# The shared network's first products moved between the last weightings and the tables, in TensorE's order

## The reference, cut to what matters

```python
xn = _layernorm(x)
# attention: softmax of masked scores, times the values
s = softmax(causal(q @ k.T / 16)) @ v
# router: softmax of 8 logits, 2 best groups of 4, then 2 best experts of those
weights, topk_idx = ...
counts = jnp.bincount(topk_idx.reshape(-1), length=E)
flat_idx = topk_idx.reshape(-1)
routed_in = xf[flat_idx] * weights
# which rows go through which expert follows from counts alone
h = silu(_grouped_mm(routed_in, w1, counts)) * _grouped_mm(routed_in, w3, counts)
routed_out = _grouped_mm(h, w2, counts)
# shared network
shared = silu(xf @ sw1.T) * (xf @ sw3.T) @ sw2.T
out = shared.at[flat_idx].add(routed_out)
x = x + s * silu(out)
```

## Time and profile before

| what | value |
|---|---|
| median of 3 runs | 239.04 us (238.71 to 239.35) |
| the profiled execution's own time | 240.62 us |
| its span, first to last instruction | 238.6 us |
| TensorE busy | 230.6 us (97%) |
| TensorE's weight loads | 205.8 us (86%) |
| VectorE, ScalarE, GpSimd busy | 186.8, 144.9, 55.4 us |
| mean granted TensorE clock | 0.993 |

### The profile page before, as it was taken

One profiled execution on the slowest core, in us unless ns is written; L12 is line 12 of the kernel. 1 busy time (PEld: TensorE's weight loads), 2 busy tenths in 40 slices (PEclk: granted clock), 3 DMA queues, 4 the chain that ended last, 5 costly groups with the idle time before them and its releaser, 6 DMA issues.

```text
span 238.6 us, 4677 instructions
## 1 busy us (share of the span) xinstructions
PE 230.6 (97%) x1533; PEld 205.8 (86%) x1533; DVE 186.8 (78%) x620; ACT 144.9 (61%) x392; POOL 55.4 (23%) x108
## 2 busy tenths in 40 slices
PE   7898999999999999999999999999999999999983
PEld 5788998998989989999899998898988889898843
DVE  3779859989899899897977985677776867869765
ACT  2444745755648457474574723779678696878722
POOL 5220631805509136073012000002020201202000
PEclk9999999999999999999999979999999999999999
DMA  5699420020200200000000000116847557393523
GB/s 156 207 326 304 157 91 1 1 87 5 88 3 0 88 3 3 0 3 0 0 3 1 0 3 0 48 26 196 142 105 197 76 145 122 103 199 57 140 74 102
DMA packets 18758, 19.45 MB, mean 82 GB/s; under 512 B 1064, under 2 KB 17712, under 8 KB 18736
## 3 DMA queue, kind: packets, MB, share of 16 engines
q1 hardware_dynamic: 15568, 16.02, 21.4%
q0 software_dynamic: 3168, 3.15, 9.1%
HBM read 14.95 MB, written 4.21 MB: 80 GB/s over the span
## 4 chain that ended last, share of the span: by engine, by line
PE 92%; DMA 2%; DVE 2%; ACT 1%; issue 1%; SPq 1%; DVEq 0%; ACTq 0%
PE bank L392 85%; PE bank L484 4%; PE bank L440 3%; DMA raw_qkv<-in_L_attn_WK 2%; DVE raw_sw L1382 1%; DVE w L1380 1%; PE bank L556 1%; PE bank L414 0%; SPq L220 0%; DVE arena L949 0%; ACT xT_hi_all L731 0%; ACT arena L731 0%; ACT probs L731 0%; ACT attn_all L731 0%; SPq L222 0%
## 5 line engine op out<-in xcount | busy, mean ns | idle before, releaser
L392 PE MATMUL bank<-xT_hi_all,arena 128*128 128x512 f32 (+3 forms) x256 | 80.7, 370 | 0.7 <-DVE arena L949 0.7
L392 PE MATMUL bank<-arena 128*128 128x256 f32 (+2 forms) x560 | 76.8, 285 | 0.3 <-ACT attn_all L731 0.3
L392 PEld LDWEIGHTS bank<-arena 128*128 128x128 f32 (+1 forms) x560 | 71.9, 186 | 5.0 <-issue 0.8
L392 PEld LDWEIGHTS bank<-xT_hi_all,arena 128*128 128x128 f32 x256 | 47.0, 189 | 8.3 <-ACT probs L761 1.4
L731 ACT ACTIVATE arena<-bank 128x512 fp32r<-128x512 f32 (+4 forms) x84 | 36.2, 452 | 24.4 <-PE bank L392 23.1
L949 DVE TENSOR_TENSOR arena<-bank,arena 128x264 fp32r<-128x264 f32 (+4 forms) x83 | 41.4, 508 | 6.9 <-ACT arena L731 6.0
L392 PE MATMUL bank<-xT_lo_all,arena 128*128 128x512 f32 (+3 forms) x128 | 45.8, 358 | 0.0
L383 POOL DMA_DIRECT2D x_ring<-in_L_attn_x x6 | 7.9, 1317 | 79.0 <-DVE x_ring L1318 79.0
L392 PEld LDWEIGHTS bank<-xT_lo_all,arena 128*128 128x128 f32 x128 | 24.2, 189 | 2.1
L731 ACT ACTIVATE attn_all<-bank,row_inv 128x256 f32<-128x256 f32 x32 | 15.2, 474 | 17.3 <-PE bank L392 15.5
L761 ACT ACTIVATE probs<-bank,neg_max 128x128 f32<-128x128 f32 (+3 forms) x32 | 17.0, 530 | 12.6 <-DVE neg_max L1008 12.5
(11 more groups left out here) (128 smaller groups left out, 381.9 us busy)
## 6 DMA issues: line engine op xcount, KB each, us to landing
x_ring<-in_L_attn_x SPq DMA_DIRECT2D x7, 512.0 KB, 3.5
x_ring<-in_L_attn_x POOLq DMA_DIRECT2D x6, 512.0 KB, 6.0
out<-x_ring SPq DMA_DIRECT2D x6, 512.0 KB, 3.3
spread<-pairs SPq DMA_DIRECT2D x14, 128.0 KB, 3.3
w_sb<-in_L_ffn_w SPq DMA_DIRECT2D x1, 1024.0 KB, 11.9
raw_sw<-in_L_ffn_sw SPq DMA_DIRECT2D x3, 256.0 KB, 4.2
x_ring<-in_L_attn_x SPq DMA_DIRECT2D x2, 256.0 KB, 2.9
xn<-in_L_attn_x SPq DMA_DIRECT2D x1, 512.0 KB, 5.3
```

Of the source, the lines that this page charges most:

```text
L392: return nc.tensor.matmul(dst, lhsT, rhs, start=start, stop=stop, skip_group_check=True, **kw)
```

## The change

Two of the four `hidden` calls of the first sequence of the second loop, both with sw1, now stand in the last sequence of the first loop: each behind a `weigh` and ahead of a `table`. The waits on `exp_done` go with them (`bank0` must have been read by the softmax of tile 2, `bank1` by that of tile 3). The two with sw3 move up: the first from behind the count to a place ahead of `table(1, 1)`, the second from behind `table(1, 3)` to a place right behind the count. Within the last sequence, `weigh(b, i)` also changes places with the tables. Nothing is added or taken out, and the other engines' lists are the same.

```diff
--- before.py
+++ after.py
@@ -569,6 +569,16 @@
                                  c == 0, c == C - 1)
                 ins.then_inc(s["tables_summed"], 1)
 
+            h1_bank, h3_bank, o_bank, bc_bank, g_bank, acc_bank = bank[0:2], bank[2:4], bank[4], bank[5], bank[6], bank[7]
+
+            def hidden(i, hc, w, dst, done):
+                b = sequence(i)
+                if i > 0:
+                    pe.wait_ge(s["h_mult_done"], C * i + hc - (C - 1))
+                hid = slice(hc * P, (hc + 1) * P)
+                split_products(dst[hc][:, :], [(swT[:, 0, w, c, hid], swT[:, 1, w, c, hid], xT_hi_all[:, b, c, :], xT_lo_all[:, b, c, :])
+                                               for c in range(C)]).then_inc(s[done], 1)
+
             scores(b, 0)
             scores(b, 1)
             turn_sw(0)
@@ -578,27 +588,22 @@
             turn_probs(b, 1)
             scores(b, 3)
             turn_sw(2)
+            weigh(b, 0)
+            pe.wait_ge(s["sw_ready"], 1)
+            pe.wait_ge(s["exp_done"], T * b + 3)
+            hidden(0, 0, 0, h1_bank, "h1_done")
             table(0, 0)
-            weigh(b, 0)
             turn_probs(b, 2)
+            weigh(b, 1)
+            pe.wait_ge(s["exp_done"], T * B)
+            hidden(0, 1, 0, h1_bank, "h1_done")
             table(0, 1)
-            weigh(b, 1)
             turn_probs(b, 3)
+            weigh(b, 2)
             table(0, 2)
-            weigh(b, 2)
             table(0, 3)
             weigh(b, 3)
 
-
-            h1_bank, h3_bank, o_bank, bc_bank, g_bank, acc_bank = bank[0:2], bank[2:4], bank[4], bank[5], bank[6], bank[7]
-
-            def hidden(i, hc, w, dst, done):
-                b = sequence(i)
-                if i > 0:
-                    pe.wait_ge(s["h_mult_done"], C * i + hc - (C - 1))
-                hid = slice(hc * P, (hc + 1) * P)
-                split_products(dst[hc][:, :], [(swT[:, 0, w, c, hid], swT[:, 1, w, c, hid], xT_hi_all[:, b, c, :], xT_lo_all[:, b, c, :])
-                                               for c in range(C)]).then_inc(s[done], 1)
 
             def routed_out():
 
@@ -655,8 +660,8 @@
             nc.tensor.transpose(x_bank[0][:, 0:P], A_T[:, :].bitcast(F32), ident[:, :]).then_inc(s["a_turned"], 1)
             table(1, 0)
             pe.wait_ge(s["sw_ready"], 3)
-            pe.wait_ge(s["exp_done"], T * B)
-            hidden(0, 0, 0, h1_bank, "h1_done")
+            pe.wait_ge(s["pT_lo"], T * B)
+            hidden(0, 0, 1, h3_bank, "h3_done")
             table(1, 1)
 
 
@@ -665,19 +670,16 @@
                 ins = mm(bc_bank[:, 0:P], ones_bf[:, :], at_least[:, :, :, :].rearrange("p t k e -> p (t k e)")[:, n * P:(n + 1) * P],
                          n == 0, n == 3)
             ins.then_inc(s["counted"], 1)
-            pe.wait_ge(s["pT_lo"], T * B)
-            hidden(0, 0, 1, h3_bank, "h3_done")
+            hidden(0, 1, 1, h3_bank, "h3_done")
             table(1, 2)
             pe.wait_ge(s["rows_ready"], 1)
             turn_pairs()
             spread_pairs(0)
-            hidden(0, 1, 0, h1_bank, "h1_done")
             pe.wait_ge(s["a_ready"], 1)
             gather(0, 0)
             spread_pairs(1)
             pe.wait_ge(s["pairs_kept"], 1)
             table(1, 3)
-            hidden(0, 1, 1, h3_bank, "h3_done")
             gather(0, 1)
             pe.wait_ge(s["attn_kept"], T * B)
             pe.wait_ge(s["b_kept"], 1)
```

## The result

The changed kernel took 247.14 us (median of 6 runs, 243.04 to 252.4) against 239.08 us for the kernel before on the same chip (238.71 to 239.35). So the change makes the kernel slower, as forecast, but by 8.1 us at the median and not by 2.8.

A forecast was written before the change was run, and what follows sets the result against it. TensorE was taken to bound the kernel, losing time to waits and a clock fall between the loops. Waits of -0.13 + 0.81 + 1.21 + 0.49 + 0.40 = +2.8 us, clock 0, on 239.04 gave 241.8 us, range 240.1 to 243.4.

The forecast's parts named there:

- The waits of `weigh(b, 1)` and of the softmax.: Last sequence of first loop: the wait of `weigh(b, 1)` goes, -0.13 us; softmax is done in time for both `hidden`, 0.
- The wait of `weigh(b, 2)`.: After the last transposes: fixed chain of 1.74 us, table moved behind, wait grows from 0.50 to 1.31; +0.81 us.
- The count is not late.: Between the loops: VectorE's routing would end at 146.9 us, TensorE reach the count at 147.6; 0.7 us slack, cost 0.
- The first gather.: Behind the count: gather can begin 4.15 us after it, TensorE has 2.94 us of work between; +1.21 us.
- The second gather.: It waits for `silu_rows(0, 0)`, 1.99 us from the first gather's start; TensorE has 1.50 us between; +0.49 us.
- The first `shared_out`.: Second loop: last low part of h comes 5.90 to 6.16 us behind the first gather; wait 0.30 to 0.56, taken as +0.40.
- The clock: TensorE's clock between the loops: falls once, as in the profiled execution, at about the same price; 0 us.
- it falls twice, or falls once where the timed runs before had none: Rival on the clock between the loops: +2.8 plus 1.2 to 1.7 us, at the middle 243.3 us; 22%.
- no fall: Rival: clock between the loops does not fall in the changed kernel, 2.8 - 1.6 = +1.2, 240.2 us; 22%.
- what stands behind the count not waited for: Rival: gathers and `shared_out` behind the count need no wait and the clock does not fall; -0.9, 238.1 us; 4%.

The follow-up runs named there:

- e1: Changed kernel, but ScalarE empties bank4 (`keep_attn(b, 1)`) ahead of `p_high(b, 3)`; 242.52 us against 238.93 for the kernel before.
- e6: Changed kernel with products of zeros filling the waits ahead of the third weighting (nine), first gather (nine) and second (three); 241.79 us against 239.17 for the kernel before.
- e11: Changed kernel with VectorE's `one_hot(0, 0)` ahead of `h_mult(0, 0)`; 244.35 us against 239.19 for the kernel before.
- e7: Changed kernel with three of four products of each table left out, so the routed part is wrong; 240.92 us against 239.17 for the kernel before.
- e10: Changed kernel with products of zeros ahead of the two gathers only (nine and three), early pause left idle; 244.93 us against 239.19 for the kernel before.
- e13: Repeat of e6 for more executions: changed kernel with zeros' products ahead of the third weighting and both gathers; 241.42 us against 239.14 for the kernel before.
- e14: Repeat of e10: changed kernel with zeros' products ahead of the two gathers only; 247.35 us against 239.14 for the kernel before.
- e5: Changed kernel with `keep_attn(b, 1)` ahead of `p_high(b, 3)` and the second half with sw1 back ahead of the first gather; 239.16 us against 239.17 before.
- e15: Changed kernel with zeros' products ahead of the gathers and `keep_attn(b, 1)` ahead of `p_high(b, 3)`; 239.88 us against 239.14 for the kernel before.
- e2: Changed kernel with one table put back between the last transposes and the third weighting; 243.57 us against 238.93 for the kernel before.
- e4: Changed kernel with the second half of the first products with sw1 put back ahead of the first gather; 242.50 us against 238.93 for the kernel before.
- e9: Changed kernel with nine products of zeros ahead of the third weighting only, gather waits left idle; 244.93 us against 239.19 for the kernel before.
- e12: The changed kernel itself, run again on another occasion; 248.50 us against 239.19 for the kernel before.
- e3: Kernel before with only the weightings and tables swapped, no `hidden` moved; 247.11 us against 238.93 for the kernel before.

## Why the prediction was right or wrong

The direction was right and the number wrong: 8.1 us instead of 2.8. Six of its seven items, the waits, came out to a few tenths; the seventh, the clock, did not. By its own items:

1. *The waits of `weigh(b, 1)` and of the softmax.* None is seen there after. Right.
2. *The wait of `weigh(b, 2)`.* 1.78 us from the transposes instead of 1.74, idle 1.14 marked. Right; +0.85 for +0.81.
3. *The count is not late.* Right: no idle time ahead of it in the changed kernel.
4. *The first gather.* At full clock in e1 the count begins at 146.03 and the gather at 150.18, in e6 at 147.82 and 151.97: 4.15 us both times, as forecast. +1.21. Only the reason was half right: `h_mult` costs 0.1 us in this chain (e11).
5. *The second gather.* 154.04 - 151.97 = 2.07 us behind the first in e6, and in e7, where nothing is filled, 151.24 - 149.17 = 2.07 too, instead of 1.99. +0.57 for +0.49.
6. *The first `shared_out`.* 157.88 - 151.97 = 5.91 us behind the first gather, at the low end of my 5.90 to 6.16; its wait is 5.91 less 5.1 of work and 0.57 of wait already taken, 0.2 (by the starts; none is marked as idle). Forecast +0.40.

The sum of the waits is -0.13 + 0.85 + 1.21 + 0.57 + 0.2 = 2.7 us. That can be held against a measurement: the seven executions with the same waits and a mean clock of 0.999 or more (e6, e10, e13, e14) have spans of 239.3 to 240.0, median 239.5, against 236.8 for the kernel before at full clock: +2.7. The forecast had 2.8.

7. *The clock* is the step that failed: forecast 0, measured 8.1 - 2.7 = 5.4 us. I took "one fall, as now, at about the same price: 0", and as the worst a second fall of 1.7 us. Two things were wrong in it. First, "as now" was read from the one profiled execution; 45 of 55 executions before have no fall to speak of, so the median of before had nothing in it that the changed kernel could keep. I had seen that the profiled execution lay 1.6 us above the median, just the price of a fall, and gave the case 22%. Second, the length of a fall was taken as the 3.41 us of the earlier trace rows. In the changed kernel the low stretch lasted 17.06 us in the profiled execution, and low time was 4.3 to 24.9 us. What ended it after 3.41 us before is not shown: the long weighting and the long products that stood behind it there stand inside the stretch of 17.06 us here (145.34, and two whole `hidden`, from 149.82 and from 154.44) and did not end it. At 0.45 us of span each that is 2 to 11 us; for the two executions in the middle of the first six (7.7 and 20.8 us) it is 3.5 and 9.4, on average 6.4. With 2.7 us of waits that makes 9.1 for the 8.1 measured. The line itself starts at 238.8 us at no low time, 2.0 above the kernel before and not 2.7, so the split between waits and clock is known to some 0.7 us.

What makes the clock fall is shown by the fillings and by e5 and e15: the two long pauses (1.14 and 0.94 us marked as idle, 1.3 and 1.2 by the starts) amid tables, small products and short weightings. Filling them (e6, e13) or removing them (e5, e15) keeps the clock in 22 executions out of 22, all on one chip; with one or both left, 38 of 42 executions have 3.4 us of low time or more (the changed kernel, e1, e2, e4, e9 to e12, e14), and on the chip of the 22 four of six (e14); so have all seven of e7. The swap of weightings and tables is enough for the whole loss (e3, 247.11 us); the `hidden` moved without the swap were not run. That the tables lengthen the low stretch is shown by e7 only as far as none of its seven executions had more than 7.6 us of low time. Why a stretch lasts as long as it does, and why e9 fell early although its pause was filled, stays open.

The sentence with the Trainium skill: by "TensorE: Matmul & The Clock Gate" (Why this matters for your kernels) pauses this short should cost no clock, and the result would have been +1.2 us. The runs contradict it: pauses of 1.14 and 0.94 us with tables and small products around them were enough, since filling them took the falls away. The measurement decides.

Of the rivals, "it falls twice, or falls once where the timed runs before had none" was the true one in kind, and far too small. The two fast cases (no fall; what stands behind the count not waited for) did not come.

## What to carry to other kernels

A wait of TensorE can cost more than its own length: here the waits added 2.7 us and the clock that fell behind two of them up to 11 us more, since it went to half and stayed there. Before work is moved away from a wait that it covers, look at each wait it uncovers (here: ScalarE's chain from the transposes to the third weighting, and the count's chain to the gather). Taking the waits out (e5) gave the time of the kernel before; where they stayed, even useless products in them took 5 to 7 us off. And read the granted clock of every timed run, not of the profiled one alone, before a fall in it is taken for the usual state.

## What the runs showed of the hardware

- The executions of one kernel that runs on one core spread over 4% (243.04 to 252.4 us), in step with their low time of 4.3 to 24.5 us.
- 1.15 us of matmuls on zeros in each of two pauses, and 0.49 in a third, held the clock in seven executions (e6, e13); the first filling alone did not (e9).
- A low stretch of 17.06 us ran through matmuls without a pause (17.06 us busy), long 128x512 products among them, and one of 23.89 us with 22.95 busy; the latter is e12's:

```profile
141.88:165.77 23.89, 22.95 (x92) 20.31 (x92) 12.00 (x37) 9.79 (x26) 0.00 (x0) 0.50 0.07 13
```
